# Key, query and value parts: from copies through DRAM to copies within SBUF

## The chip, the cores and the metric

The kernel runs on one core of one Trainium2 chip. The metric is the device time of one execution in microseconds (us), median of several runs. Engines are named TensorE (PE in the profile, its weight loads PEld), VectorE (DVE), ScalarE (ACT), GpSimd (POOL) and SyncE (SP); SyncE here does nothing but issue DMAs, in one order written out by hand.

## The reference, cut to what matters

32 items of 128 x 512 numbers go through a cross attention along the 512 positions (8 heads of 16 channels, keys and values from a second input) and then through a mixture of 8 experts with 2 chosen per token, plus a shared expert:

```
x   = x + tanh(g0) * attention(layernorm(x), ctx)     # per item: q, k, v = W @ x; scores over 512 x 512 per head;
                                                      # softmax; weighted values; 128 channels x 512 positions
x   = x + tanh(g1) * (moe(rmsnorm(layernorm(x))) + shared(rmsnorm(layernorm(x))))
```

The change is in the attention alone.

## The kernel before, in words

**Turns.** The attention runs in turns i = -3 to 31 (`TURNS`); an item is b. In turn i TensorE computes the transposed scores of item i (`exp_scores`, L882: 32 steps of four matmuls), their weighted sum with the values (`values`, L913), and, for item i+1, a first set of scores whose only use is the row maxima (`max_scores`, L860: 16 pairs of matmuls). VectorE takes the maxima of each pair (`maximum`, L1129), ScalarE the exponentials (`exponential`, L1413). Between them, at fixed steps s of the 32, lie the projections of item i+3 (`project`, L838; its value part, L844, is that of item i+2), their evacuation (`evacuate`, L1396 and L1400), the turning of the tokens of item i-3 and their router logits. All engines follow written orders and meet through semaphores; nothing is reordered at run time.

**Parts.** Keys and queries are cut into three bfloat16 parts, high, middle and low (`high_part` on ScalarE at steps 27 and 31 of turn b-3; the two others in `split` on GpSimd, L671 to L674: keys of item b near the end of turn b-3, queries at the start of turn b-2). The scores are one matmul over stacked parts: rows 0 to 47 of `k_stack` and `q_stack` hold 16 channels x 3 parts, and rows 64 to 111 the other three products; rows 32 to 63 hold also the constants and the maxima. Three stacks of each kind rotate (`b % 3`). [...]

**The way through DRAM.** `write` (L444) stores parts in `parts_d`: two DMAs of 256 KB for keys and two for queries per item. `read` (L458) loads them into the stacks: four DMAs of 192 KB for each. `max_scores` waits at its first step for all eight reads (`s_rd`). The maxima of an item come back as two rows of the query stack in `row` (L520), for half 0 before the turn of the item, for half 1 within it.

**The weighted values.** `take_values` (L1421) copies the sums of four heads, 16 value rows and 16 equal rows of denominators each, to `pv_sb`; `store_values` (L467) writes all 512 KB to `pv_d`, `spread_denominators` (L474) spreads four rows on 64 partitions for the reciprocal (`invert`), `store_reciprocals` (L478) writes them to DRAM, and `load_values` reads them back broadcast (L485) with the value rows (L486). `add_attention` on GpSimd (L681 to L683) waits for both.

**SyncE's order in turn i**, before: write(i+2, queries, HI); row(i, 1); spread_denominators(i-1); store_values(i-1); read(i+2, keys); write(i+2, queries, MID with LO); load_ctx, store_turned, load_x; row(i+1, 0); store_reciprocals(i-1); read(i+2, queries); load_values(i-1); store_tokens(i-2); store_staged, load_staged; write(i+3, keys, HI, then MID with LO). These are 28 DMAs. After the last turn come 71 jobs of matrix products, 32 of the shared expert and 39 of chosen ones (L956), which the change doesn't touch apart from the last item's values in jobs 0 to 4.

Of the kernel before, what the change touches and what calls it, by code (L numbers as in the profile page):

```python
# [7 lines left out]
F32 = mybir.dt.float32  # L8
# [20 lines left out]
STORED = ((LO, MID, HI, HI), (HI, HI, MID, LO))  # L29
HELD = ((HI, LO, MID), (HI, MID, LO))  # L30
FIRST_AT, SECOND_AT = (1, 0), (0, 1)
READS = 8
WRITES = 2
# [56 lines left out]
def build(nc, x_d, ctx_d, g_xattn_d, g_ffn_d, wq_d, bq_d, wk_d, bk_d, wv_d, bv_d, rms_d, router_d, w_d, out_d):  # L90
# [6 lines left out]
    with es:  # L97
# [50 lines left out]
        parts = [[held[n][:, HELD[n].index(part), :] for part in (HI, MID, LO)] for n in range(2)]  # L148
# [107 lines left out]
        parts_d = [[dram(f"parts_{n}{i}", (4, DH, HEADS, L), BF16) for i in range(2)] for n in "kq"]  # L256
        pv_d = dram("pv_d", (HEADS, 2 * DH, L), F32)
# [25 lines left out]
        s_wr = [sem(f"s_wr{i}") for i in range(2)]  # L283
        s_rd = [sem(f"s_rd{i}") for i in range(3)]
# [9 lines left out]
        s_w = sem("s_w")  # L294
# [102 lines left out]
        def lane(v, a):  # L397
            return v.rearrange("p (g a j) l -> p a g (j l)", g=2, a=2)[:, a, :, :]

        @block.sync  # L400
        def _(sp):
# [33 lines left out]
            def write(b, n, part):  # L435
                if b >= 2 and part == HI:
                    sp.wait_ge(s_rd[(b - 2) % 3], READS * DMA * ((b - 2) // 3 + 1))
                if part == HI:
                    sp.wait_ge(s_hi, 2 * b + n + 1)
                else:  # L440
                    sp.wait_ge(s_part, 4 * b + 2 * n + 2)
                rows = parts_d[n][b % 2].rearrange("t d h l -> (d h) t l")
                at = STORED[n].index(part if part == HI else HELD[n][1])
                sp.dma_start(rows[:, at:at + 2, :],  # L444
                             parts[n][HI].unsqueeze(1).broadcast_to([P, 2, L]) if part == HI else held[n][:, 1:3, :]
                             ).then_inc(s_wr[n], DMA)

            def read(b, n):
                sp.wait_ge(s_wr[n], WRITES * DMA * (b + 1))
                if b >= 3 and n == 0:  # L450
                    sp.wait_ge(s_es, STEPS * (b - 2))
                if b < 3 and n == 0:
                    sp.wait_ge(s_blank[b], 2)
                src = parts_d[n][b % 2]
                stack = (k_stack, q_stack)[n][b % 3]
                for a in range(2):
                    for row, at in ((LANE * a, FIRST_AT[n]), (LANE * (1 - a), SECOND_AT[n])):
                        sp.dma_start(lane(stack[row:row + STACK, :, :], a),  # L458
                                     lane(src[at:at + 3].rearrange("t d h l -> (t d) h l"), a)
                                     ).then_inc(s_rd[b % 3], DMA)  # L460

            def store_values(b):
                sp.wait_ge(s_u, 2 * b + 2)
                sp.wait_ge(s_fin, 2 * DMA * b)
                sp.dma_start(pv_d.rearrange("(g h) e l -> (h e) g l", g=2), pv_sb).then_inc(s_w, DMA)  # L467

            def spread_denominators(b):
                sp.wait_ge(s_u, 2 * b + 2)  # L470
                if b:
                    sp.wait_ge(s_rc, b)
                for g in range(2):
                    sp.dma_start(den_c[P // 2 * g:P // 2 * (g + 1), :], pv_sb[DH:P:2 * DH, g, :]).then_inc(s_sc, DMA)  # L474
# [5 lines left out]
            def load_values(b):  # L480
                sp.wait_ge(s_r, DMA * (b + 1))
                sp.wait_ge(s_w, DMA * (b + 1))
# [3 lines left out]
                sp.dma_start(pv_num, pv_d[:, 0:DH, :]).then_inc(s_fin, DMA)  # L486
# [36 lines left out]
            for i in TURNS:  # L523
                if is_b(i + 2):
                    write(i + 2, 1, HI)
# [1044 lines left out]
```

## Time and profile before

| | |
|---|---|
| median of 3 runs | 1391.8 us (1387.26, 1391.97, 1391.8) |
| the profiled execution | 1386.7 us, its span 1384.8 us |
| mean granted clock of TensorE | 0.983 of full speed |
| busy share: PE, DVE, ACT, POOL | 93%, 70%, 63%, 62% |
| DMA: MB moved, mean rate | 256.65 MB, 185 GB/s |
| DMA queue of SyncE | 149102 packets, 217.08 MB, 59.0% of 16 engines |

A busy TensorE is not TensorE at its peak, since matmuls are pipelined and their ends are modelled; so the waits say more than the share. Start times in the rows are us from the start of the span. A wait for several semaphores is put down to the one that came last.

### The profile page before, as it was taken

The numbers are of one execution on the slowest core, as the hardware profiler recorded it, in microseconds if no ns is written. First come the engines' busy times: TensorE is split into PE (matmuls) and PEld (weight loads), VectorE is DVE, ScalarE is ACT, GpSimd is POOL, SyncE is SP. The second block draws the span as 40 slices with busy tenths as digits, with TensorE's granted clock in tenths as the row PEclk, the third lists the DMA queues.
The fourth block names the chain that finished last, engine by engine and source line by source line (L and its number), as shares of the span: only waits on it lengthen the run. The fifth ranks groups of instructions, "written<-read, shape, count | busy, mean of one in ns | idle before, by whom it ended". The sixth has DMA issues, their size and how long they took to land.

```text
span 1384.8 us, 34397 instructions
## 1 busy us (share of the span) xinstructions
PE 1288.3 (93%) x12274; PEld 682.2 (49%) x12274; DVE 975.1 (70%) x1661; ACT 871.8 (63%) x1720; POOL 861.5 (62%) x1267
## 2 busy tenths in 40 slices
PE   2899999999999999999999989799999999999997
PEld 0233333333333333333333323587788888888886
DVE  5989889999999998989999877457654333333332
ACT  2488888888888888888888768333334333333332
POOL 8647777678787878877887643442114555555553
PEclk7799999999999999999999999999999999999999
DMA  7677887778888888788888773676555998885665
GB/s 187 185 197 227 224 241 220 207 227 214 201 223 207 213 218 227 191 222 210 218 217 221 162 185 90 161 161 149 127 175 105 214 216 193 178 189 110 108 110 81
DMA packets 167522, 256.65 MB, mean 185 GB/s; under 512 B 31717, under 2 KB 65132, under 8 KB 167358
## 3 DMA queue, kind: packets, MB, share of 16 engines
q1 hardware_dynamic: 149102, 217.08, 59.0%
q0 software_dynamic: 18256, 37.38, 14.9%
q8 instruction: 103, 1.69, 0.5%
q14 instruction: 61, 0.50, 0.1%
HBM read 141.06 MB, written 112.27 MB: 183 GB/s over the span
## 4 chain that ended last, share of the span: by engine, by line
PE 61%; DVE 12%; issue 10%; DMA 7%; POOL 3%; ACT 3%; SPq 2%; POOLq 1%; DVEq 0%; ACTq 0%
PE m_banks L956 21%; PE bank L913 12%; PE bank L882 10%; DVE row_max L1129 8%; PE m_banks L860 7%; PE bank L838 3%; PE bank L888 3%; DMA arena<-parts_q 2%; PE bank L844 2%; ACT arena L1413 2%; DMA arena<-ht_d 1%; POOL xs L780 1%; PE bank L978 1%; SPq L458 1%; PE bank L869 1%
## 5 line engine op out<-in xcount | busy, mean ns | idle before, releaser
L1129 DVE TENSOR_REDUCE row_max<-m_banks 128x2 f32<-128x1024 f32 x512 | 615.0, 1222 | 76.1 <-PE m_banks L860 67.9
L1413 ACT ACTIVATE arena<-bank 128x512 f32<-128x512 f32 x1024 | 552.4, 606 | 73.4 <-PE bank L882 71.9
L882 PE MATMUL bank<-arena 112*32 112x512 bf16 x4096 | 336.2, 382 | 6.6 <-ACT arena L1413 3.2
L913 PE MATMUL bank<-arena 128*32 128x512 f32 x2048 | 280.2, 598 | 0.4 <-ACT arena L1421 0.3
L882 PEld LDWEIGHTS bank<-arena 112*32 112x32 bf16 x4096 | 114.7, 95 | 266.0 <-ACT arena L1413 132.4
L792 POOL DMA_INDIRECT out<-xs,ids x71 | 112.3, 1582 | 173.4 <-ACT xs L1495 135.7
L860 PE MATMUL m_banks<-arena 48*128 48x512 bf16 x1024 | 177.4, 393 | 39.6 <-DVE row_max L1129 25.7
L956 PE MATMUL m_banks<-w_ring,h_hi 128*128 x568 | 183.0, 403 | 0.0
L1484 ACT ACTIVATE arena<-m_banks 128x256 f32<-128x256 f32 x103 | 39.5, 384 | 186.9 <-PE m_banks L956 186.9
L860 PEld LDWEIGHTS m_banks<-arena 48*128 48x128 bf16 x1024 | 40.4, 93 | 175.2 <-DVE row_max L1129 79.9
L1337 DVE TENSOR_TENSOR arena<-arena,m_banks 128x256 f32<-128x256 f32 x71 | 29.9, 421 | 116.5 <-ACT arena L1484 116.5
L956 PE MATMUL m_banks<-w_ring,h_lo 128*128 x284 | 111.7, 393 | 0.0
L956 PEld LDWEIGHTS m_banks<-w_ring,h_hi 128*128 128x128 f32 x568 | 101.4, 189 | 18.4
L671 POOL TENSOR_TENSOR arena<-arena 128x512 bf16<-128x512 f32 x62 | 72.2, 1165 | 49.8 <-ACT arena L1405 46.7
L1331 DVE TENSOR_TENSOR act_lo<-bank,act_hi 128x256 fp32r<-128x256 f32 x71 | 30.1, 424 | 96.7 <-ACT act_hi L1501 96.7
L681 POOL TENSOR_TENSOR arena<-arena 128x512 f32<-128x512 f32 x32 | 40.9, 1277 | 89.9 <-DMA arena<-pv_d 86.9
L780 POOL DMA_INDIRECT xs<-h_d,ids x71 | 70.2, 989 | 41.0 <-issue 21.0
L732 POOL DMA_INDIRECT map_d<-meta,slots x64 | 65.5, 1023 | 47.2 <-DVE slots L1216 31.4
L1495 ACT ACTIVATE xs<-m_banks,wts 128x512 f32<-128x512 f32 x71 | 48.8, 688 | 71.0 <-PE m_banks L956 71.0
L913 PEld LDWEIGHTS bank<-arena 128*32 128x32 f32 x2048 | 64.8, 109 | 49.6 <-issue 26.5
L956 PE MATMUL m_banks<-w_ring,act_hi 128*128 x284 | 87.5, 389 | 1.4 <-DVE act_lo L1331 1.4
L838 PE MATMUL bank<-arena 128*32 128x512 f32 x512 | 72.1, 636 | 16.4 <-POOL arena L662 11.1
(182 smaller groups left out, 1999.9 us busy)
## 6 DMA issues: line engine op xcount, KB each, us to landing
arena<-parts_k SPq DMA_DIRECT2D x128, 192.0 KB
arena<-parts_q SPq DMA_DIRECT2D x128, 192.0 KB
parts_k<-arena SPq DMA_DIRECT2D x64, 256.0 KB, 6.6
parts_q<-arena SPq DMA_DIRECT2D x64, 256.0 KB, 5.1
pv_d<-arena SPq DMA_DIRECT2D x32, 512.0 KB, 4.3
split_d<-staged SPq DMA_DIRECT2D x30, 512.0 KB, 9.1
w_ring<-split_d SPq DMA_DIRECT2D x60, 256.0 KB, 3.9
arena<-in_w SPq DMA_DIRECT2D x36, 256.0 KB, 8.4
```

Source lines behind the costliest of these rows:

```text
L671: nc.gpsimd.tensor_tensor(mid, proj[n], hi, ALU.subtract).then_inc(s_part, 1)
L732: nc.gpsimd.indirect_dma_start(map_d, bass.IndirectOffsetOnAxis(ap=slots[:, k, b:b + 1], axis=0), meta[:, k, b, :], None).then_inc(s_sc2, DMA)
L780: nc.gpsimd.indirect_dma_start(gathered[i % IN_RING], None, h_d, bass.IndirectOffsetOnAxis(ap=ids[:, i:i + 1], axis=0)).then_inc(s_got[i % ...
L792: nc.gpsimd.indirect_dma_start(out_d, bass.IndirectOffsetOnAxis(ap=ids[:, i:i + 1], axis=0), y_sb[i % OUT_RING], None, compute_op=ALU.add) ...
L838: last = nc.tensor.matmul(out[c, :], (wk, wq)[n][:, c], ctx_in[b % 2] if n == 0 else xn[b % 2], start=True, stop=True)
L860: nc.tensor.matmul(m_ps[pair % M_PAIRS][:, a, :], q_stack[b % 3][rows, h, qt * P:(qt + 1) * P], k_stack[b % 3][rows, h, :], start=True, st ...
L882: last = nc.tensor.matmul(out[c, :], k_stack[b % 3][0:SHIFTED, h, kt * P + c.start:kt * P + c.stop], q_stack[b % 3][0:SHIFTED, h, :], star ...
L913: last = nc.tensor.matmul(pv_ps[2 * DH * j:2 * DH * (j + 1), :], v_ones[b % 3][:, kt, GROUP * g + j, :], probs[pair % 3][:, j, :], start=( ...
L956: last = nc.tensor.matmul(out, v[:, c, :], weights(j, part, first_row + c), start=(c == 0 and n == 0), stop=(c == chunks - 1 and n == 2))
L1129: nc.vector.reduce_max(pair, m_ps[(STEPS * b + u) // 2 % M_PAIRS], AX_X).then_inc(s_mx, 1)
L1413: nc.scalar.activation(probs[group % 3][:, j, :], bank_of["scores", b, s], ACT.Exp, scale=float(DH) ** -0.5).then_inc(s_exp, 1)
L1495: nc.scalar.activation(y_sb[i % OUT_RING], Y_PS[j % 2], ACT.Copy, scale=wts[:, i:i + 1]).then_inc(s_yrt, 1)
```

## The change

Each part is copied straight from where `split` and `high_part` leave it into the rows of the stacks. The stacks interleave the three parts of a channel now (every third row), so each copy writes 16 partitions, 3 apart, x 8 or 4 heads x 512. Keys take 10 copies an item and queries 8: six of 128 KB and twelve of 64 KB. All of an item's are issued in turn b-2: the high key parts first of all in the turn, the rest after `spread_denominators`. The value rows and rows of ones of `v_ones` alternate, and `send_values` copies the 128 value rows (2 x 128 KB) straight to `pv_num`; the 512 KB store and the 256 KB load are gone. The reciprocals go through DRAM as before. `parts_d` and `pv_d` are gone. Neighbouring heads (a) lie on the two halves of the partitions now, where pairs of heads did.

```diff
-READS = 8
-WRITES = 2
+SLOTS_OF = (((HI, HI), (HI, MID), (MID, LO)), ((HI, LO), (MID, MID), (HI, HI)))
+COPIES = tuple(sum(2 if first == second else 4 for first, second in slots) for slots in SLOTS_OF)
...
+            def copy_parts(b, n, part):
                 if part == HI:
+                    if n == 0:
+                        if b >= 3:
+                            sp.wait_ge(s_es, STEPS * (b - 2))
+                        if b < 3:
+                            sp.wait_ge(s_blank[b], 2)
                     sp.wait_ge(s_hi, 2 * b + n + 1)
+                if part == MID:
                     sp.wait_ge(s_part, 4 * b + 2 * n + 2)
+                stack, src = (k_stack, q_stack)[n][b % 3], parts[n][part]
+                for at, (first, second) in enumerate(SLOTS_OF[n]):
+                    for base in (0, LANE):
+                        rows = stack[base + at:base + at + STACK - 2:len(SLOTS_OF[n]), :, :]
+                        if part == first == second:
+                            sp.dma_start(rows, src).then_inc(s_cp[n], DMA)
+                        else:
+                            for a in range(2):
+                                if part == (first if base == LANE * a else second):
+                                    sp.dma_start(rows[:, a:HEADS:2, :], src[a:P:2, :]).then_inc(s_cp[n], DMA)
+
+            def send_values(b):
                 sp.wait_ge(s_u, 2 * b + 2)
+                if b:
+                    sp.wait_ge(s_x2, b)
+                for g in range(2):
+                    sp.dma_start(pv_num[P // 2 * g:P // 2 * (g + 1), :], pv_sb[0:P:2, g, :]).then_inc(s_num, DMA)
...
             for i in TURNS:
                 if is_b(i + 2):
-                    write(i + 2, 1, HI)
+                    copy_parts(i + 2, 0, HI)
                 if is_b(i):
                     row(i, 1)
                 if is_b(i - 1):
                     spread_denominators(i - 1)
-                    store_values(i - 1)
                 if is_b(i + 2):
-                    if i + 2 > 0:
-                        read(i + 2, 0)
-                    write(i + 2, 1, MID)
-                    if i + 2 == 0:
-                        read(0, 0)
+                    copy_parts(i + 2, 0, MID)
+                    copy_parts(i + 2, 0, LO)
+                    for part in (HI, MID, LO):
+                        copy_parts(i + 2, 1, part)
+                if is_b(i - 1):
+                    send_values(i - 1)
...
                 if is_b(i - 1):
                     store_reciprocals(i - 1)
-                if is_b(i + 2):
-                    read(i + 2, 1)
                 if is_b(i - 1):
-                    load_values(i - 1)
+                    load_reciprocals(i - 1)
...
-                if is_b(i + 3):
-                    for part in (HI, MID):
-                        write(i + 3, 0, part)
...
             def split(b, n):
...
-                pool.wait_ge(s_wr[n], WRITES * DMA * b)
+                pool.wait_ge(s_cp[n], COPIES[n] * DMA * b)
...
             def add_attention(b):
-                pool.wait_ge(s_fin, 2 * DMA * (b + 1))
+                pool.wait_ge(s_num, 2 * DMA * (b + 1))
+                pool.wait_ge(s_fin, DMA * (b + 1))
...
             def max_scores(b, u):
                 if u == 0:
-                    pe.wait_ge(s_rd[b % 3], READS * DMA * (b // 3 + 1))
+                    for kind in range(2):
+                        pe.wait_ge(s_cp[kind], COPIES[kind] * DMA * (b + 1))
...
             def evacuate(b, n):
-                        act_e.wait_ge(s_wr[n], WRITES * DMA * b)
+                        act_e.wait_ge(s_cp[n], COPIES[n] * DMA * b)
...
-                nc.scalar.copy(v_ones[b % 3][:, :, :, 0:DH],
+                nc.scalar.copy(v_ones[b % 3][:, :, :, 0::2],
```

## Rows read from the trace of the kernel before

**Rows 1.** The page: busy time by engine, and the chain that ended last.
```profile
PE 1288.3 (93%) x12274; PEld 682.2 (49%) x12274; DVE 975.1 (70%) x1661; ACT 871.8 (63%) x1720; POOL 861.5 (62%) x1267
...
PE 61%; DVE 12%; issue 10%; DMA 7%; POOL 3%; ACT 3%; SPq 2%; POOLq 1%; DVEq 0%; ACTq 0%
```

**Rows 2.** Windows: opening, turns 5 to 28, and a half-clock stretch of turn 30.
```profile
core 0: us, PE busy (x) PEld busy (x) DVE busy (x) ACT busy (x) POOL busy (x), PEclk, DMA share, GB/s
...
12.50:14.00 1.50, 0.66 (x4) 0.20 (x8) 0.00 (x0) 0.00 (x0) 1.42 (x3) 1.00 1.06 377
20.50:31.50 11.00, 1.99 (x10) 0.29 (x12) 3.47 (x17) 1.30 (x2) 9.11 (x21) 0.50 0.95 199
826.10:832.90 6.80, 5.91 (x38) 1.76 (x42) 3.14 (x5) 2.38 (x5) 1.70 (x2) 0.50 0.60 173
174.20:823.50 649.30, 613.34 (x7801) 219.16 (x7797) 592.48 (x950) 532.13 (x1028) 501.70 (x830) 1.00 0.81 212
```

**Rows 3.** Waits over turns 5 to 28: total us, times, longest.
```profile
PEld bank L882 <- ACT arena L1413: 97.1, 300, 0.5
...
POOL arena L681 <- DMA arena<-pv_d: 42.4, 21, 5.3
...
PEld bank L882 <- DMA arena<-m_rows: 3.9, 5, 1.9
PE m_banks L860 <- DMA arena<-parts_q: 3.0, 2, 1.5
```

**Rows 4.** The same view over the whole run.
```profile
PE m_banks L860 <- DMA arena<-parts_q: 13.2, 5, 6.5
```

**Rows 5.** Timeline of TensorE where turns 4, 5 and 21 begin.
```profile
149.14 0.61 PE L882 MATMUL bank<-arena 112*32 112x512 bf16 x8
...
174.24 0.61 PE L882 MATMUL bank<-arena 112*32 112x512 bf16 x8
...
589.36 0.62 PE L882 MATMUL bank<-arena 112*32 112x512 bf16 x8
591.46 0.61 PE L860 MATMUL m_banks<-arena 48*128 48x512 bf16 x4 [1.49 <-DMA arena<-parts_q]
```

**Rows 6.** The chain that ended last, opening: start us, us, what.
```profile
18.76 0.36 SPq L444
...
24.35 7.05 DMA arena<-parts_q
...
45.02 0.56 SPq L520
```

**Rows 7.** Timeline of the opening: TensorE, then GpSimd.
```profile
23.02 1.94 PE L838 MATMUL bank<-arena 128*32 128x512 f32 x8 [5.03 <-POOL arena L662]
31.44 1.04 PE L860 MATMUL m_banks<-arena 48*128 48x512 bf16 x4 [6.49 <-DMA arena<-parts_q]
...
51.84 0.61 PE L882 MATMUL bank<-arena 112*32 112x512 bf16 x8
53.29 0.61 PE L860 MATMUL m_banks<-arena 48*128 48x512 bf16 x4 [0.85 <-DMA arena<-parts_q]
...
32.62 1.15 POOL L674 TENSOR_TENSOR arena<-arena 128x512 bf16<-128x512 f32 x1
...
36.34 1.15 POOL L674 TENSOR_TENSOR arena<-arena 128x512 bf16<-128x512 f32 x1
```

**Rows 8.** Timeline of SyncE's DMA queue in turn 20: start us, us.
```profile
568.17 1.20 SPq L520 DMA_DIRECT2D arena<-m_rows  x2
...
571.71 3.33 SPq L458 DMA_DIRECT2D arena<-parts_k  x4
...
580.21 1.17 SPq L520 DMA_DIRECT2D arena<-m_rows  x2
...
582.04 3.07 SPq L458 DMA_DIRECT2D arena<-parts_q  x4
585.23 0.65 SPq L485 DMA_DIRECT2D arena<-rden_d  x1
```

More of the change, by code:

```diff
@@ L147, in build @@
         held = [a.take(3 * L // 2, BF16).rearrange("p (t l) -> p t l", t=3) for _ in range(2)]
-        parts = [[held[n][:, HELD[n].index(part), :] for part in (HI, MID, LO)] for n in range(2)]
+        parts = [[held[n][:, part, :] for part in (HI, MID, LO)] for n in range(2)]
         wq, wk, wv = (a.take(P) for _ in range(3))
@@ L253, in build @@
         bank_of = {}
-        parts_d = [[dram(f"parts_{n}{i}", (4, DH, HEADS, L), BF16) for i in range(2)] for n in "kq"]
-        pv_d = dram("pv_d", (HEADS, 2 * DH, L), F32)
         rden_d = dram("rden_d", (HEADS, L), F32)
@@ L282, in build @@
         s_part = sem("s_part")
-        s_wr = [sem(f"s_wr{i}") for i in range(2)]
-        s_rd = [sem(f"s_rd{i}") for i in range(3)]
+        s_cp = [sem(f"s_cp{i}") for i in range(2)]
         s_ms = sem("s_ms")
@@ L441, in write @@
                     sp.wait_ge(s_part, 4 * b + 2 * n + 2)
[L442 to L460, printed above, removed]
@@ L473, in spread_denominators @@
                 for g in range(2):
-                    sp.dma_start(den_c[P // 2 * g:P // 2 * (g + 1), :], pv_sb[DH:P:2 * DH, g, :]).then_inc(s_sc, DMA)
+                    sp.dma_start(den_c[P // 2 * g:P // 2 * (g + 1), :], pv_sb[1:P:2 * DH, g, :]).then_inc(s_sc, DMA)
             def store_reciprocals(b):
@@ L478, in store_reciprocals, with load_reciprocals @@
                 sp.dma_start(rden_d, rden_c).then_inc(s_r, DMA)
-            def load_values(b):
+            def load_reciprocals(b):
                 sp.wait_ge(s_r, DMA * (b + 1))
-                sp.wait_ge(s_w, DMA * (b + 1))
                 if b:
@@ L741, in _ @@
             for n in (1, 2):
-                link(nc.gpsimd.memset(v_ones[n][:, :, :, DH:], 1.0))
+                link(nc.gpsimd.memset(v_ones[n][:, :, :, 1::2], 1.0))
                 nc.gpsimd.memset(middle_rows(k_stack[n]), TWO_ONES).then_inc(s_blank[n], 1)
@@ L858, in max_scores @@
                 for a in range(2):
-                    rows, h = slice(LANE * a, LANE * a + STACK), GROUP * g + 2 * a + j
+                    rows, h = slice(LANE * a, LANE * a + STACK), GROUP * g + 2 * j + a
                     nc.tensor.matmul(m_ps[pair % M_PAIRS][:, a, :], q_stack[b % 3][rows, h, qt * P:(qt + 1) * P],
@@ L1127, in maximum @@
                 half, w = divmod(u // 2, GROUP * KT // 2)
-                pair = row_max[b % 2][:, GROUP * KT * half:GROUP * KT * (half + 1)].rearrange("p (a w) -> p w a", a=2)[:, w, :]
+                pair = row_max[b % 2][:, GROUP * KT * half:GROUP * KT * (half + 1)].rearrange("p (j a t) -> p j t a", a=2, t=KT)[:, w // KT, w % KT, :]
                 nc.vector.reduce_max(pair, m_ps[(STEPS * b + u) // 2 % M_PAIRS], AX_X).then_inc(s_mx, 1)
@@ L1144, in _ @@
             nc.vector.memset(middle_rows(k_stack[0]), TWO_ONES).then_inc(s_blank[0], 1)
-            nc.vector.memset(v_ones[0][:, :, :, DH:], 1.0).then_inc(s_ones, 1)
+            nc.vector.memset(v_ones[0][:, :, :, 1::2], 1.0).then_inc(s_ones, 1)
             run(moments(0))
@@ L1418, in take_values @@
                 if b:
-                    act_e.wait_ge(s_w, DMA * b)
+                    act_e.wait_ge(s_num, 2 * DMA * b)
                     act_e.wait_ge(s_sc, 2 * DMA * b)
```

19 lines of the change are left out of this document (3 added, 16 removed).

## The prediction, made before the change was run

> **What bounds the kernel now.** The page comes first. TensorE is busy 93% of the span and has 61% of the chain that ended last, while DMA as a whole has 7% of that chain [rows 1]. So taking traffic away pays only where a transfer is what TensorE waits for. The window of turns 5 to 28 sizes the attention: 802 exponentials were counted there, or 25.06 turns in 649.3 us, which makes 25.91 us a turn, and TensorE is busy in 613.34 us of it [rows 2]. A turn without a disturbance, turn 4, takes 174.24 - 149.14 = 25.10 us [rows 5]. The DMA engines are busy 0.81 of that window at 212 GB/s [rows 2]: nearly full, and yet seldom waited for. The waits tell why. In 25 turns TensorE waits 97.1 us for exponentials in small pieces, which is the pace of the turn itself, but only 3.0 us for query parts, and its weight loads wait 3.9 us for maxima rows [rows 3]. The reader is to see that steady turns are set by the interplay of TensorE, ScalarE and VectorE. Over the whole run the wait for query parts is 13.2 us in 5 cases [rows 4]. The opening holds two of them: 6.49 us before turn -1's first maxima matmul at 31.44, and 0.85 us at 53.29 [rows 7]. Turn 21 has one of 1.49 [rows 5], another of that size makes up the 3.0, and 13.2 - 6.49 - 0.85 - 3.0 leaves 2.9 us for a later one, at turn 30. The removal of these waits is what the change can bring.
>
> **The opening.** The last query parts of item 0 exist at about 18.7: their store is issued at 18.76. Key reads, then query reads follow, the last issued at 24.35, and it lands 7.05 us later [rows 6]. The copies need no second trip. High query parts go ahead of that time; after 18.76 four copies are left, at 0.6 us an issue (x2 in 1.20, x4 in 3.33 or 3.07 with some crowding [rows 8]), so the last is issued at about 21.2. Queries are 768 KB; at the 199 GB/s of the stretch 20.5 to 31.5, where these very stack rows are written from DRAM [rows 2], that takes 3.9 us and is paced by the issues. I take a landing by 24.5. TensorE is then not ready either: the projection at 23.02 ends at 24.96 and itself waited for GpSimd [rows 7]. Turn -1's maxima start at 25.0 instead of 31.44: 6.4 us won. With the old 7.05 us of landing it would be 28.3, and 3.1 us.
>
> Turn -1 is then a row of maxima on VectorE, unchanged. It would put the start of turn 0 at 45.4 instead of 51.84. Its first scores need row(0, 0). That was issued at 45.02 when the maxima were there [rows 6], which becomes 38.6, but now eighteen copies of item 1 stand ahead of it in SyncE's order. GpSimd finishes item 1's key parts at 33.8 and its query parts at 37.5 [rows 7], times that don't move, since its work there is continuous. Six key copies run to 37.4, four high query copies to 39.8, four more to 42.2, load_ctx to 42.9; the row goes out by 44.1 and I take 2 us to land: 46.1, 0.7 us after the start it could have had (between 0 and 3). The 0.85 us wait for item 1 goes. TensorE's granted clock was half from 20.5 to 31.5 [rows 2]; where it returns moves with the work, and I charge 1 us, between 0 and 3.4: half of the 6.8 us that one half-clock stretch lasted [rows 2]. Opening: 6.4 + 0.85 - 0.7 - 1.0 = 5.6 us won, bounds 0 and 7.3.
>
> **Steady turns.** Before, the last query read of turn 20 ends its issue at 585.11, about 4 us before the next turn at 589.36, whose first maxima wait for it [rows 5, 8]. The copies are issued in one block: high keys at 0 to 2.4 us of the turn, row(i, 1) at 4 as before, the denominators to 6.5, fourteen copies to 15 or 16. The last goes out some 5 us before the old one did. The waits of 3.0 + 2.9 = 5.9 us fall away; at worst they stay. The maxima rows stand behind less traffic: of their 3.9 us I take half, 2.0 (0 to 3.9).
>
> Traffic: 1.05 MB of stores, 0.5 MB of value stores and 0.26 MB of loads go; 1.57 MB of reads turn into copies of as many bytes and 0.26 MB of value copies come. The stores ran at 377 GB/s [rows 2], so some 4 us of 21 us of DMA time a turn are freed. Nothing waits for that time by itself. GpSimd's 42.4 us for pv_d [rows 3] shrink, since only the reciprocals are left to wait for. GpSimd is off the path: I count 0. The upper bound is half of what turns 5 to 28 hold above 25.10 us after the waits named: (0.81 x 25 - 6.9) / 2 = 6.7 us.
>
> The new stops. The copies have a new place in `evacuate`: ScalarE must wait until all of the previous item's copies have landed, with the exponentials queued behind it and TensorE behind those. The query evacuation is at step 29, about 22.8 us of the turn; copies issued by 16 have 6 us and more to land. Cost nothing while that cover stands. The writes with stride 2 into `v_ones` have the same 512 elements a row, and I count 0. No row has the stride. If it doubled such a copy, that would be 532.13 / 1028 = 0.52 us a turn on an engine that is idle (649.30 - 532.13) / 25 = 4.7 us of each [rows 2], so 0 to 0.5 us a turn, and I take the lower end.
>
> **The issue queue.** SyncE had 28 DMAs a turn and gets 28 - 12 - 2 + 18 + 2 = 34. At 0.6 us that is 20.4 instead of 16.8 us. Waits that remain: 1.6 us for the maxima before row(i, 1), and now the landing of the reciprocals. The query reads used to lie in that gap, and 582.0 to 585.23 sufficed [rows 8], so at most 3.2 us. 20.4 + 1.6 + 3.2 = 25.2 against 25.9: it fits, but barely. row(i+1, 0) goes out some 2 us later than its 16 us of the turn, and still has 6.
>
> A rule of the Trainium skill speaks against this cut into pieces: "SBUF — State Buffer", section on the DMA setup-cost knee, has small transfers dominated by a fixed part, 64 KB moving at about 138 GB/s. By an estimate from that page, twelve such copies and six of 128 KB take some 10 us a turn, about what stores and reads took together, and it would not change the sum. No row of before has such a copy.
>
> **The sum.** 5.6 + 5.9 + 2.0 = 13.5 us. The profiled execution took 1386.7 (span 1384.8), so it would be 1373.2. The median of the runs is 5.1 us above the profiled time; against 1391.8 it is 1378.3, and I say 1378. Its own range, from the bounds: 1368 to 1386.
>
> **Rivals.** *Only the opening pays.* The late waits are an accident of how DMAs fell in three turns, and others come in their place, for a maxima row or a landing. For it: two of the three lie among the last turns, where shared weights are loaded too. Against: the copies lead by 5 us. Time: 1391.8 - 5 = 1387, within 0.5%. Chance 0.20.
>
> *SyncE becomes the bound* (the other side). An issue of a copy with two strided sides could take longer than 0.6; the four reads took up to 0.83 each in 571.71 [rows 8]. The room is 0.7 us, and the wait of 1.6 us would shrink before the turn grows, so it decides from 0.6 + 2.3 / 18 = 0.73 us a copy; each further 0.1 adds 1.8 us a turn. At 0.83 that is 1.8 x 28 turns = 50, less the 13.5: 1428. For it: how little room there is. Against: an average of 0.6 for transfers with as many dimensions. Chance 0.11.
>
> *The copies clog the DMA engines.* A turn moves 212 x 25.91 = 5.5 MB; without stores, reads and value traffic, and with the value copies, 2.35 MB are left, 6.2 us at 377 GB/s. The copies would have to fall from 199 to under 1.57 / 19.7 = 80 GB/s to fill the turn. Neither a 1 KB piece (the stores had them, at 377) nor the stack rows (199) come near. At 70 GB/s: 2.7 us x 28 = 76, less 13.5: 1454. Chance 0.06.
>
> **How the numbers follow.** The forecast has 0.63. Faster by over 0.5% means under 1384.8; 7 us is what this measurement can tell from none, with runs 4.7 us apart. Nearly all of the forecast is that (0.60), and a small part of the first rival (0.04): 0.64. Same: 0.03 and 0.15, so 0.18. Slower: 0.17 and a little of the first rival: 0.18. The range must leave out at most 2 in 10: 1368 to 1395, which leaves the two slow rivals outside.
>
> **What would show it.** Right: no L860 wait on a DMA at turns 21, 29, 30; the first L860 at about 25; turn 0 near 46; SyncE's row(i+1, 0) at 18 us of a turn; 32 x 1.57 = 50 MB less moved; GpSimd's L681 waiting little. Wrong: copy issues above 0.7 us; L520 released late, followed by L882 waiting for m_rows; L1396 waiting for a DMA; a turn mean above 25.9; half clock in turn 0.

## The result: 8% slower, and the profile after

The changed kernel takes 1502.6 us, the median of 4 runs (1498.6 to 1506.3), against 1389.5 for 4 runs of the kernel before: a ratio of 1.080 [1.076, 1.085]. The profiled execution took 1498.57 us with a span of 1496.7, at a mean granted clock of 0.947 where before had 0.983.

The page of the kernel after: span, busy time by engine, the DMA totals, the chain that ended last, and one of the costliest groups (busy us and mean ns, then idle time before it, and from what).

```profile
span 1496.7 us, 34532 instructions
...
PE 1328.1 (89%) x12274; PEld 682.8 (46%) x12274; DVE 976.7 (65%) x1661; ACT 875.2 (58%) x1720; POOL 860.3 (57%) x1267
...
DMA packets 154468, 206.34 MB, mean 138 GB/s; under 512 B 35046, under 2 KB 84845, under 8 KB 154303
...
PE 40%; SPq 26%; DMA 10%; issue 10%; DVE 7%; POOL 5%; ACT 2%; POOLq 1%; ACTq 0%; DVEq 0%
...
L1401 ACT COPY arena<-bank 128x512 f32<-128x512 f32 x64 | 37.3, 583 | 103.3 <-DMA arena<-arena 102.1
```

The traffic did what was said: 256.65 MB became 206.34, so 50.3 MB are gone. Every engine does the work that it did before [rows 1]; TensorE's busy time is 3.1% longer, 39.8 us for the same instructions at a lower mean clock; the others' is within 0.4%. The other 72.1 of the 111.9 us between the spans are standing time of TensorE. In the chain TensorE fell from 61% to 40% and SyncE's queue rose from 2% to 26%. The last row names the place: ScalarE's 64 copies in `take_values` have 102.1 us of idle time in front of them, released by DMAs between buffers on chip.

The window view of the kernel after, of its exponentials alone (32 a turn): turns 5 to 28, turn 15, and a stretch of turn 17.

```profile
core 0: us, ACT busy (x), PEclk, DMA share, GB/s
193.38:916.00 722.62, 413.01 (x768) 0.94 0.47 132
497.50:525.50 28.00, 17.59 (x34) 1.00 0.55 152
578.00:584.50 6.50, 2.67 (x5) 0.50 0.37 121
```

The first row holds 768 exponentials, so 24 turns, in 722.62 us: 30.11 us a turn, where before it was 25.91 [rows 2]. Turn 15 takes 28.00 us at full clock. The last row is a stretch at half clock, begun 20 us into turn 17, and 17 of the 24 turns have one. The seven others take 27.8 to 28.5 us, 28.1 on average; the 17 average (722.6 - 7 x 28.1) / 17 = 30.9. Of the 4.2 us that a turn has grown, 2.2 are there without any half clock, and 2.0 come with it.

The attention holds the whole loss. The last four exponentials of turn 31 start in the timeline of ScalarE after at:

```profile
990.47 2.06 ACT L1393 ACTIVATE arena<-bank 128x512 f32<-128x512 f32 x4 [3.09 <-PE bank L862]
```

Before, the row is:

```profile
873.48 2.06 ACT L1413 ACTIVATE arena<-bank 128x512 f32<-128x512 f32 x4 [2.80 <-PE bank L882]
```

That is 117.0 us later. Behind it each kernel has some 510 us left (1384.8 - 873.5 = 511.3, 1496.7 - 990.5 = 506.2), so the jobs give back 5 us, and 117.0 - 5.1 is the 111.9 us between the two spans.

**Where a turn stands still.** The waits of the kernel after from 174 to 900 us, some 24 turns (total us, times, longest):

```profile
POOL arena L649 <- ACT arena L1385: 148.1, 24, 11.3
...
PE bank L893 <- ACT arena L1401: 87.2, 24, 5.1
ACT arena L1401 <- DMA arena<-arena: 85.0, 24, 5.0
```

No maxima matmul waits for a transfer any more, as forecast [rows 3, 4]. But ScalarE waits 85.0 us in 24 turns for a copy between buffers, 3.5 us on average and 2.6 to 5.0 in each, and TensorE's value matmuls wait 87.2 us for ScalarE. One wait passes through to the other whole. GpSimd's wait follows from it: it stands idle until ScalarE has made the next high part, later in the turn than before. Turn 15, which starts at 497.5, shows how it comes about. SyncE's queue in the timeline (start us, us):

```profile
501.40 1.18 SPq L503 DMA_DIRECT2D arena<-m_rows  x2
502.67 1.25 SPq L459 DMA_DIRECT2D arena<-arena  x2
503.97 5.08 SPq L445 DMA_DIRECT2D arena<-arena  x8
509.09 3.14 SPq L441 DMA_DIRECT2D arena<-arena  x4
512.27 1.25 SPq L445 DMA_DIRECT2D arena<-arena  x2
513.62 1.17 SPq L452 DMA_DIRECT2D arena<-arena  x2
...
516.44 1.22 SPq L503 DMA_DIRECT2D arena<-m_rows  x2
517.70 0.58 SPq L463 DMA_DIRECT2D rden_d<-arena  x1
521.94 0.66 SPq L469 DMA_DIRECT2D arena<-rden_d  x1
...
524.66 3.34 SPq L441 DMA_DIRECT2D arena<-arena  x2
```

The order of the turn can be read down the list. The maxima row goes out 3.9 us into the turn, when VectorE has it, then `spread_denominators` (L459), fourteen part copies until 513.5, and only then `send_values` (L452). Behind those come the three 256 KB transfers, row(16, 0), and `store_reciprocals` (L463). The load of the reciprocals (L469) starts 3.66 us after that store's issue ended, and the next turn's high keys at 524.66. The same turn on ScalarE, and then on TensorE:

```profile
513.89 0.60 ACT L1393 ACTIVATE arena<-bank 128x512 f32<-128x512 f32 x1 [1.15 <-PE bank L862]
517.09 0.59 ACT L1401 COPY arena<-bank 128x512 f32<-128x512 f32 x1 [2.60 <-DMA arena<-arena]
...
517.82 1.06 PE L893 MATMUL bank<-arena 128*32 128x512 f32 x8 [2.69 <-ACT arena L1401]
```

ScalarE was free at 514.49, 17.0 us into the turn. Its next instruction is `take_values(15, 0)` at step 20. This overwrites `pv_sb`, from which `send_values(14)` reads, and those two copies were issued at 513.62 and landed at about 517.0. ScalarE stands for 2.60 us, exponentials of the steps behind it are queued on the same engine, and TensorE stands for 2.69. The next turn then starts later by about that much: turn 15 takes 28.0 us, turn 4 before took 25.1 [rows 5]. SyncE's order, which is tied to the turn's start by row(i, 1), moves with it, and the wait is met again in every turn from 1 to 29: 102.1 us in all. Turn 15 is one of the milder cases.

### The profile page after: what moved, and what is told of

Its sections match the earlier page's. It is cut to its first block, busy times and chain, and to the rows that moved or that the text cites. A ratio compares the mean times of both kernels' runs of the same rounds, so it can differ in the third digit from the quotient of the medians.

```text
span 1496.7 us, 34532 instructions
## 1 busy us (share of the span) xinstructions
PE 1328.1 (89%) x12274; PEld 682.8 (46%) x12274; DVE 976.7 (65%) x1661; ACT 875.2 (58%) x1720; POOL 860.3 (57%) x1267
## 2 busy tenths in 40 slices
DMA packets 154468, 206.34 MB, mean 138 GB/s; under 512 B 35046, under 2 KB 84845, under 8 KB 154303
## 4 chain that ended last, share of the span: by engine, by line
PE 40%; SPq 26%; DMA 10%; issue 10%; DVE 7%; POOL 5%; ACT 2%; POOLq 1%; ACTq 0%; DVEq 0%
PE m_banks L936 20%; SPq L445 14%; PE bank L893 6%; SPq L441 6%; DMA arena<-arena 5%; PE bank L862 5%; PE bank L817 4%; DVE row_max L1109 4%; PE m_banks L840 3%; SPq L503 2%; SPq L459 2%; DMA rden_d<-arena 2%; SPq L452 2%; PE bank L868 1%; DMA arena<-rden_d 1%
## 5 line engine op out<-in xcount | busy, mean ns | idle before, releaser
L893 PE MATMUL bank<-arena 128*32 128x512 f32 x2048 | 294.8, 629 | 105.0 <-ACT arena L1401 104.9
L862 PE MATMUL bank<-arena 112*32 112x512 bf16 x4096 | 349.3, 395 | 8.9 <-ACT arena L1393 5.8
L862 PEld LDWEIGHTS bank<-arena 112*32 112x32 bf16 x4096 | 119.1, 98 | 295.1 <-ACT arena L1393 155.1
L817 PE MATMUL bank<-arena 128*32 128x512 f32 x512 | 86.0, 752 | 15.9 <-POOL arena L640 10.6
L840 PEld LDWEIGHTS m_banks<-arena 48*128 48x128 bf16 x1024 | 37.1, 95 | 137.3 <-issue 87.8
L1401 ACT COPY arena<-bank 128x512 f32<-128x512 f32 x64 | 37.3, 583 | 103.3 <-DMA arena<-arena 102.1
L1311 DVE TENSOR_TENSOR act_lo<-bank,act_hi 128x256 fp32r<-128x256 f32 x71 | 30.1, 424 | 96.7 <-ACT act_hi L1481 96.7
L711 POOL DMA_INDIRECT map_d<-meta,slots x64 | 65.3, 1021 | 47.3 <-DVE slots L1196 30.9
```

What stands on the lines that cost most here:

```text
L817: last = nc.tensor.matmul(out[c, :], (wk, wq)[n][:, c], ctx_in[b % 2] if n == 0 else xn[b % 2], start=True, stop=True)
L840: nc.tensor.matmul(m_ps[pair % M_PAIRS][:, a, :], q_stack[b % 3][rows, h, qt * P:(qt + 1) * P], k_stack[b % 3][rows, h, :], start=True, st ...
L862: last = nc.tensor.matmul(out[c, :], k_stack[b % 3][0:SHIFTED, h, kt * P + c.start:kt * P + c.stop], q_stack[b % 3][0:SHIFTED, h, :], star ...
L893: last = nc.tensor.matmul(pv_ps[2 * DH * j:2 * DH * (j + 1), :], v_ones[b % 3][:, kt, GROUP * g + j, :], probs[pair % 3][:, j, :], start=( ...
```

## The experiments

The ratios are to the kernel before, measured beside each run; the intervals are 95%. None leaves work out; three add some. A maxima row that is late is waited for by the weight loads and then by the matmuls behind them; the two rows of a view overlap, so they are not added up. First came the place of `send_values` in the order, with one edit each: 0, 6 or 10 part copies ahead of it in its block instead of 14.

### Values first

```diff
                 if is_b(i - 1):
                     spread_denominators(i - 1)
+                    send_values(i - 1)
...
-                if is_b(i - 1):
-                    send_values(i - 1)
```

> The value copies stand right behind the spreading of the denominators instead of behind fourteen part copies; nothing else differs from the changed kernel. Theory A (their place: ScalarE's first taking of values in a turn waits for the value copies of the item before to land): that taking returns from about 20 to about 17 us of a turn, a turn takes 25.5 to 26.5 us, the kernel 1375 to 1400 us. Theory B (SyncE has too many issues, 34 a turn): the order changes nothing, 1470 to 1505 us. Theory C (copies within SBUF are slow in the DMA engines): likewise above 1470 us, with landings of parts far above 3 us.

Measured: 1388.2 us, ratio 1.002 [0.999, 1.004]. ScalarE's wait for copies is gone, and with it the loss of 8%. A turn takes 26.6 us on average in turns 5 to 28, a little more than expected. It may not be the best place: SyncE itself stands 20.8 us in 14 turns for GpSimd, which still reads `pv_num`, and TensorE's weight loads wait 18.0 us for maxima rows.

### Values after the key copies, and after ten copies

```diff
                     copy_parts(i + 2, 0, MID)
                     copy_parts(i + 2, 0, LO)
-                    for part in (HI, MID, LO):
-                        copy_parts(i + 2, 1, part)
                 if is_b(i - 1):
                     send_values(i - 1)
+                if is_b(i + 2):
+                    for part in (HI, MID, LO):
+                        copy_parts(i + 2, 1, part)
```

> The value copies stand behind six part copies (the middle and low key parts), 3.7 us later than in the run with none ahead. Theory A: they are issued at 10 to 11 us of the turn and land by 14, before step 20 at about 16.5, so the time is that of the run with none ahead, within 8 us. Were every place in the queue worth its 0.62 us, it would be 6 x 0.62 x 28 = 104 us above that one. Theories B and C: about 1500 us, as the changed kernel.

Measured with six copies ahead: 1383.7 us, ratio 0.996 [0.994, 0.999].

The next one puts the four high query copies ahead of `send_values` as well:

```diff
                     copy_parts(i + 2, 0, LO)
+                    copy_parts(i + 2, 1, HI)
                 if is_b(i - 1):
                     send_values(i - 1)
                 if is_b(i + 2):
-                    for part in (HI, MID, LO):
+                    for part in (MID, LO):
                         copy_parts(i + 2, 1, part)
```

> The value copies stand behind ten part copies. Theory A: issued by 14 us of the turn, landing at about 16.5, at the edge: 0 to 1 us a turn, so 0 to 28 us above the run with six ahead, where fourteen ahead cost over 100 us. The cost is a threshold, not a slope from the first copy. Theories B and C: about 1500 us.

Measured with ten ahead: 1404.8 us, ratio 1.012 [1.008, 1.015]. Its wait of `take_values` for copies, over 174 to 850 us:

```profile
ACT arena L1403 <- DMA arena<-arena: 38.0, 22, 4.4
```

In the same stretch the wait is 0 with none ahead, 3.4 us with six, 38.0 with ten and 82.5 with fourteen, at ratios of 1.002, 0.996, 1.012 and 1.080. The traffic, the copies and the number of issues are the same in all four. That leaves the order as the cause. The four copies from six to ten cost 2.5 us of issue each turn, and six copies ahead is about where the landing meets its user just in time. The time lost is not in proportion to the wait: from six to ten copies 34.6 us more of it go with 21 us, from ten to fourteen 44.5 with 98.

### A second buffer, with the order of the change

```diff
+        second_half = arena[:, a.at:a.at + L]
...
+        def pv_half(b, g):
+            return second_half if g == 0 and b % 2 else pv_sb[:, g, :]
...
             def take_values(b, g):
-                if b:
-                    act_e.wait_ge(s_num, 2 * DMA * b)
-                    act_e.wait_ge(s_sc, 2 * DMA * b)
-                nc.scalar.copy(pv_sb[:, g, :], pv_ps).then_inc(s_u, 1)
+                sent = b if g else b - 1
+                if sent > 0:
+                    act_e.wait_ge(s_num, 2 * DMA * sent)
+                    act_e.wait_ge(s_sc, 2 * DMA * sent)
+                nc.scalar.copy(pv_half(b, g), pv_ps).then_inc(s_u, 1)
```

> The changed kernel in its own order, the value copies behind fourteen part copies, but the first half of the weighted values of odd items goes to a second buffer, so that the taking at step 20 waits only for the copies of two items before. Theory A (the wait of ScalarE on that landing is the cost, not the late issue): the waits of ScalarE on a DMA vanish, 1378 to 1400 us. Theory B (the queue as such is too long) or C: stays above 1450 us. Waits for maxima rows may remain and make up 10 to 20 us.

`send_values` stays behind fourteen copies. Only the first half of an odd item's values goes to another buffer, so that the taking at step 20 has to wait for the item before the last one. Measured: 1386.0 us, ratio 0.996 [0.993, 0.999]. `take_values` waits for no DMA. This settles it: with the issue order of the change untouched, taking away what makes ScalarE wait takes the 8% away. What is late instead (174 to 850 us):

```profile
POOL arena L664 <- DMA arena<-rden_d: 86.0, 23, 8.6
...
PEld bank L866 <- DMA arena<-m_rows: 26.1, 14, 6.4
...
PE bank L866 <- DMA arena<-m_rows: 16.8, 9, 5.5
```

GpSimd waits 86.0 us for the reciprocals, and TensorE's weight loads wait 26.1 us for maxima rows, with the matmuls' 16.8 inside that. Even so the kernel ends 0.4% under the one before.

### The two halves of the change alone

Values through DRAM again, at the old place and with the old store and load; parts by copies (34 issues a turn):

```diff
                 if is_b(i - 1):
                     spread_denominators(i - 1)
+                    store_values(i - 1)
...
-                if is_b(i - 1):
-                    send_values(i - 1)
```

> Only the parts go by copies within SBUF; the weighted values go through DRAM, with their store at its old place and their load behind that of the reciprocals. SyncE has 34 issues a turn, as in the changed kernel. Theory A: ScalarE waits only for the early store, so a turn takes 25.5 to 26.5 us and the kernel 1375 to 1400 us. Theory B (34 issues are too many): about 1500 us. Theory C: about 1500 us.

Measured: 1379.7 us, ratio 0.996 [0.993, 0.999], against 1385.9 beside it.

The kernel before, with only the values by copies, in the place of its store (28 issues):

```diff
                 if is_b(i - 1):
                     spread_denominators(i - 1)
-                    store_values(i - 1)
+                    send_values(i - 1)
```

> The kernel before, with only the weighted values sent by copies within SBUF, at the place where their store stood. 28 issues a turn, as before. Values direct by themselves gain nothing, since no wait of TensorE hung on them: 1378 to 1392 us, same as before within 0.5%. If ScalarE's stop on the landing of the values were costly wherever they stand, it would show here too: above 1400 us.

Measured: 1388.0 us, ratio 0.998 [0.995, 1.001]. Neither half is slow by itself. The parts alone bring 6 us, about the opening, and the values alone nothing that can be told from none.

### The clock kept up through the wait

```diff
+            def keep_busy(b, u, count):
+                pair = (STEPS * b + u) // 2
+                pe.wait_ge(s_mx, pair - M_PAIRS + 1)
+                for _ in range(count):
+                    nc.tensor.matmul(m_ps[pair % M_PAIRS][:, 0, :], q_stack[b % 3][0:STACK, 0, 0:P],
+                                     k_stack[b % 3][0:STACK, 0, :], start=True, stop=True)
...
+                    if s == 20 and is_b(i) and i and is_b(i + 1):
+                        keep_busy(i + 1, s + GROUP, 14)
```

> The changed kernel with 14 added matmuls (48 rows, 128 x 512, 3 us at full clock) in each turn right ahead of the weighted values at step 20, where TensorE stands waiting; their results are overwritten. In the changed kernel 22 of 31 turns held 3.4 or 6.8 us at half clock and took 30 to 33 us, those without took 27.8 to 28.5. If the clock is half of the loss: half-clock time in the turns falls from 126 us to under 20, turns to 28.0 to 28.8, the kernel 1440 to 1460 us. If the clock costs nothing beside the wait, the added work is hidden or added: 1500 us or up to 30 us more.

The order is the change's; fourteen matmuls whose result is overwritten stand where TensorE would wait. Measured: 1501.6 us, ratio 1.079 [1.074, 1.083]: by the number the second expectation, though the clock did come back in part. TensorE's timeline in such a turn:

```profile
510.37 3.19 PE L847 MATMUL m_banks<-arena 48*128 48x512 bf16 x14 [0.59 <-DVE row_max L1118]
513.87 1.06 PE L900 MATMUL bank<-arena 128*32 128x512 f32 x8 [0.31 <-ACT arena L1410]
```

The gap is filled: 0.59 and 0.31 us of idling stand where turn 15 had 2.69, and no turn from 1 to 30 has a gap of TensorE over 1.1 us. ScalarE's wait stays (80.8 us). The mean granted clock rises from 0.947 to 0.961 only, and the time not at all. If the clock is at one of its two levels, its half-speed share is 2 x (1 - mean): 159 us of the span after, 117 here, 47 before. The added matmuls took back 42 us of half clock; in turns 0 to 30 it is 92 us of 126, where the first expectation had under 20. In turns 5 to 28 those without any half clock take 28.9 us on average instead of 28.1, and the mean over all 24 is 30.2 instead of 30.1: the added work costs what the clock gives back. The clock still fell in 17 of the turns 1 to 30, so TensorE's standing is not what it needs to fall.

The lengths of the turns within this run price the half clock. Against the 11 without it (28.9 us), the 6 with a stretch of 3.4 us take 1.5 us more and the 7 with 6.8 us take 3.1 more, so about half its length. By that, an estimate, the 92 us of half clock in turns 5 to 28 of the changed kernel are worth some 42 us, 1.8 of the 4.2 us that a turn has grown. It compares turns and is not a test of its own.

Nor does the length of a wait decide: in the changed kernel the clock stayed at full behind 3.33 us of standing in turn 21 and fell behind 2.62 in turn 3.

### Does the number of issues matter by itself?

The kernel before with six tiny DMAs more a turn (34, as after):

```diff
                     write(i + 2, 1, MID)
...
+                    for k in range(6):
+                        sp.dma_start(extra_d[i + 2, k], ident[0:16, 0:8]).then_inc(s_extra, DMA)
```

> The kernel before with six more DMAs of 512 bytes a turn (34 issues, as many as the changed kernel), issued right behind the store of the middle query parts; they write to DRAM what nobody reads. If 34 issues are too many for SyncE in themselves: every turn grows and the kernel takes more than 1450 us. If they fit and only what stands behind them comes later (the maxima rows by up to 1 us, the query reads by some): 1388 to 1410 us.

Measured: 1418.7 us, ratio 1.022 [1.018, 1.026]. Its waits for the query parts (174 to 850 us):

```profile
PEld m_banks L866 <- DMA arena<-parts_q: 24.4, 16, 5.6
...
PE m_banks L866 <- DMA arena<-parts_q: 19.1, 13, 5.1
```

The matmuls' 19.1 us lie within the weight loads' 24.4; before had 5.9 and 7.8 in the same stretch. The time lies between the two expectations, above 1410 and far below 1450. The six issues took 2.80 us of the queue in one turn, and before had less room than that in front of its last reads. So issues do cost, when they stand ahead of something that is needed soon.

### An order that puts what is late first

Six copies, `send_values`, six query copies, `store_reciprocals`, the last two query copies, row(i+1, 0), `load_reciprocals`, and only then the three 256 KB transfers:

```diff
                 if is_b(i + 2):
-                    for part in (HI, MID, LO):
-                        copy_parts(i + 2, 1, part)
+                    copy_parts(i + 2, 1, HI)
+                    copy_parts(i + 2, 1, MID)
+                if is_b(i - 1):
+                    store_reciprocals(i - 1)
+                if is_b(i + 2):
+                    copy_parts(i + 2, 1, LO)
+                if is_b(i + 1):
+                    row(i + 1, 0)
+                if is_b(i - 1):
+                    load_reciprocals(i - 1)
                 if is_b(i + 4) and i + 4 >= 2:
                     load_ctx(i + 4)
...
-                if is_b(i + 1):
-                    row(i + 1, 0)
-                if is_b(i - 1):
-                    store_reciprocals(i - 1)
-                if is_b(i - 1):
-                    load_reciprocals(i - 1)
```

> Against the order with the values behind six part copies: the reciprocals are stored before the last two query copies, the maxima rows of the next item go out right behind those copies, and the loads of context and x and the store of turned tokens come last. What the run with six ahead still showed was TensorE waiting 10.7 us for maxima rows over 25 turns and GpSimd 61 us for reciprocals. Theory A with this remainder (the 34 issues fit, the urgent ones must stand first): the waits for maxima rows fall under 3 us, the turn mean to 25.7 to 26.1 us, the kernel 1368 to 1378 us. Theory B in its weak form (34 issues with copies are at their limit whatever the order): the waits only move elsewhere and the time stays at 1380 to 1388 us.

Measured: 1366.3 us, ratio 0.982 [0.979, 0.985]: faster than both kernels, 24.6 us below before and 9% below the change. That is a little better than expected, but not for the reason given: the weight loads' wait for maxima rows did not fall under 3 us, it is 10.3 where the order with six ahead has 7.7. SyncE's own waits, first of the kernel after (174 to 850 us):

```profile
SPq L469 <- DMA rden_d<-arena: 79.0, 22, 8.1
SPq L503 <- DVE m_rows L1119: 31.1, 20, 2.4
```

and of this one:

```profile
SPq L503 <- DVE m_rows L1122: 54.9, 27, 6.0
...
SPq L469 <- DMA rden_d<-arena: 0.5, 1, 0.5
```

The 79.0 us in which the whole queue stood for the reciprocals' way through DRAM are 0.5, since two copies and the row are issued meanwhile. The only long wait left is for the maxima themselves, as before.

Two runs asked which of the moves brings it. This order differs from the one with six ahead in three places: the store of the reciprocals, their load, and row(i+1, 0). Only the row moved, from the order with six copies ahead:

```diff
                         copy_parts(i + 2, 1, part)
+                if is_b(i + 1):
+                    row(i + 1, 0)
...
-                if is_b(i + 1):
-                    row(i + 1, 0)
```

> The order with the values behind six part copies, and one more move: the maxima rows of the next item are issued before the loads of context and x and the store of turned tokens instead of behind them; the reciprocals stay where they were. If the rows' lateness (10.7 us of TensorE's waits over 25 turns) was what kept that version at 0.9963 of the time before: most of the way to the reordered version, 1368 to 1376 us. If the reciprocals' way (61 us of GpSimd's waits, and the query parts that GpSimd makes later for it) was: 1378 to 1386 us.

Measured: 1415.8 us, ratio 1.018 [1.014, 1.021], against both expectations. The store of the reciprocals now stands directly behind the three 256 KB transfers. SyncE waits for it before the next turn's work, and row(i, 1) of that turn is late, 12 to 15 us in:

```profile
SPq L469 <- DMA rden_d<-arena: 74.5, 18, 7.2
```

```profile
PEld bank L863 <- DMA arena<-m_rows: 22.7, 12, 3.3
...
PE bank L863 <- DMA arena<-m_rows: 12.9, 10, 2.3
```

Only the store of the reciprocals moved:

```diff
+                    copy_parts(i + 2, 1, HI)
+                    copy_parts(i + 2, 1, MID)
+                if is_b(i - 1):
+                    store_reciprocals(i - 1)
+                if is_b(i + 2):
+                    copy_parts(i + 2, 1, LO)
```

> The order with the values behind six part copies, with one move: the reciprocals are stored before the last two query copies instead of behind the maxima rows; their loading, the rows and the loads of context and x stay where they were. In the version without this move SyncE stood 55.7 us over 25 turns waiting for the reciprocals to land in DRAM, and moving the rows alone made it 1416 us. If that round trip is what bound the queue: SyncE's wait for it falls under 5 us, the kernel comes to 1362 to 1374 us, the time of the fully reordered version. If both moves are needed: 1376 to 1386 us.

Measured: 1392.5 us, ratio 1.005 [1.002, 1.009], again against both. SyncE no longer waits for the reciprocals, but row(i+1, 0) still stands behind the 256 KB transfers, and TensorE waits for it:

```profile
PEld bank L865 <- DMA arena<-m_rows: 31.2, 14, 5.2
...
PE bank L865 <- DMA arena<-m_rows: 21.2, 9, 4.3
```

By their ratios, one move alone costs 2.1% or 0.9% against the order that it started from (0.996), 30 or 13 us; both, with the load of the reciprocals moved as well, win 1.5%, 20 us. I did not foresee that. The waits suggest why: each alone leaves something needed soon behind the big transfers. They are not the whole of it, since the row moved also went with 34 us of half clock in turns 5 to 28, where six ahead has 3. The two moves without that of the load were not run, so how much of the gain is the load's is open.

The last run gives the good order six tiny DMAs more a turn (40), ahead of `send_values`:

```diff
                     copy_parts(i + 2, 0, LO)
+                    for k in range(6):
+                        sp.dma_start(extra_d[i + 2, k], ident[0:16, 0:8]).then_inc(s_extra, DMA)
                 if is_b(i - 1):
                     send_values(i - 1)
```

> The reordered version with six more DMAs of 512 bytes a turn, 40 issues, placed between the key copies and the value copies; they write to DRAM what nobody reads. SyncE's own time becomes 40 x 0.62 = 25 us of a turn of 25.7. Theory of a full queue: all stands later by 3.7 us, the values land at the edge of step 20 and the maxima rows after it: a turn of 27 to 28 us, the kernel 1400 to 1440 us. If SyncE's issues cost nothing as long as the order is right: under 1380 us.

Measured: 1459.4 us, ratio 1.049 [1.045, 1.053], above what was expected. The first wait is back (174 to 850 us):

```profile
ACT arena L1410 <- DMA arena<-arena: 44.7, 24, 3.8
```

Pushing the value copies back by some 2.8 us brings ScalarE's wait again, with something else than part copies ahead of them. It does not price that wait: 38.0 us of it with ten copies ahead went with 21 us over six ahead, and here 93 us are lost. Weight loads also wait 27.2 us for rows, and how much is due to the count of 40 is left open.

## Why the prediction was wrong, step by step

**The opening: right.** TensorE's timeline after:

```profile
22.95 1.94 PE L817 MATMUL bank<-arena 128*32 128x512 f32 x8 [4.58 <-POOL arena L640]
24.81 1.04 PE L840 MATMUL m_banks<-arena 48*128 48x512 bf16 x4
...
46.58 0.62 PE L862 MATMUL bank<-arena 112*32 112x512 bf16 x8 [0.89 <-DMA arena<-m_rows]
```

The first maxima matmul starts at 24.81 (said: 25.0; before 31.44 [rows 7]) with nothing to wait for, since the projection ends just then. Turn 0 starts at 46.58 (said: 46.1), 0.89 us of it waiting for row(0, 0) (said: 0.7), and 5.3 us before the old one (said: 5.6 with the clock's part).

**The waits for parts: right.** None is left, neither in the turns nor at turns 29 and 30. Whether their 5.9 us became time cannot be read from the changed kernel. The parts alone brought 6.2 us of 1385.9 in all, and 5.1 of it is the opening (turn 0 at 46.76).

**The price of an issue: right, within 7%.** Of turn 15's copies eight took 5.08 us and two 1.25, so 0.62 to 0.64 us each. The fourteen were out 16.0 us into the turn (said: 15 or 16). The copies land fast; from the page of the kernel after (KB, median us from issue to landing):

```profile
arena<-arena SPq DMA_DIRECT2D x256, 128.0 KB, 2.9
arena<-arena SPq DMA_DIRECT2D x384, 64.0 KB, 2.1
```

So they did not clog the DMA engines; that rival is out. The Trainium skill ("DMA: Bandwidth & Descriptors", the section on the anatomy of one DMA, on the path of DMAs that GpSimd issues) gives each transfer a fixed part of about 2.0 us, mostly the write's receipt, and bytes at 436 GB/s on top. These copies are issued by SyncE. By an estimate from that page 64 KB take 2.15 us, near the 2.1 of the row, and 128 KB 2.3, which is 0.6 too little here.

**The new stops: the step that failed.** The prediction named one new wait of a compute engine for landings, that of `evacuate`, and gave it 6 us of cover. That cover stood: in the changed kernel `evacuate` waits for no copy; only with 40 issues a turn does it, 7.8 us in 5 cases. Its stride of 2 into `v_ones` is real but small, 646 ns a copy where before had 586. But the prediction never named the other wait that the diff shows, that of `take_values` for `s_num`. Before, the 512 KB store of the values was issued ahead of the parts, and its landing covered; the change puts the copies that replace it behind fourteen others. The prediction's own numbers would have priced it: copies out by 16 us, 1.2 us of issue for `send_values`, some 2 us of landing, so 19.2 us at the earliest. In turn 20 of the kernel before TensorE begins and ScalarE takes the values at:

```profile
564.11 0.80 PE L882 MATMUL bank<-arena 112*32 112x512 bf16 x8
```

```profile
580.71 0.58 ACT L1421 COPY arena<-bank 128x512 f32<-128x512 f32 x1
```

That is 16.6 us into the turn, so the wait would have come out at 2.6 us a turn, 73 us over the 28 turns that the prediction counts with. It measured 3.5 us on average, 102.1 in all; that turn 15 shows just 2.60 is luck. The half clock comes on top, by the estimate above. The prediction asked "who waits" of the parts and GpSimd's `pv_num`, but not of the buffer that the copies read from: the program lets nobody overwrite the source of a copy before it has landed.

**The issue queue: a size too small, and a wrong place to look.** The landing of the reciprocals was bounded at 3.2 us. SyncE's wait for it is 79.0 us in 22 cases, 3.6 on average and 8.1 at most. The sum of 25.2 us against 25.9 still said "it fits", and it did in the sense meant: the rival in which the price of SyncE's issues sets the turn was not the loss, since SyncE itself has 7 us of waits a turn (79.0 + 31.1 above, with 29.0 and 24.0 for two others, over 22.5 turns). Whether the queue is full says little. What decides is when its order reaches each transfer that has a user with a fixed time.

**The maxima rows and GpSimd.** With the loss in place TensorE hardly waited for a row. Without it the rows are the next thing late: the weight loads wait 7.7 us with six copies ahead, 10.3 reordered, 22.7 with the row moved, 26.1 with the second buffer, 31.2 with the early reciprocals, where before had 3.9. The forecast had 2.0 us won there. GpSimd was taken as without price. No run tests that, but its waits for the reciprocals do not follow the time: 9.3 us in the changed kernel, at 1.080, and 86.0 with the second buffer at 0.996.

**The range.** "From the bounds" the prediction's own range goes to 1386. Its bounds give more: with nothing won in the opening and the waits left as they were, the upper end is 1391.8. The lower bound of 0 in the opening is not the sum of its terms either (3.1 won with the old landing, less up to 3 and 3.4). Neither mattered beside the wait that was left out.

**What stays open.** Why the granted clock falls 19 to 22 us into many turns, even with the gap filled. What the half clock costs by itself is an estimate from turn lengths, since the run meant to separate it from the wait did not. Where all of the reordered kernel's 24.6 us comes from is also open. In its profiled execution, itself 8.5 us above its median, the opening gives 5.6 us (turn 0 at 46.29 instead of 51.84), the turns 3 and the jobs 3 more. Its turns 5 to 28 are no shorter than before's (26.2 us on average against 26.0); turn 30 is, 23.6 against 29.0, since before had a wait and half clock there. And the saved 50 MB were never seen to pay by themselves.

## What to carry to other kernels

When a transfer is moved in a hand-written queue, list everything that waits for its landing: the reader of the target, and the engine that next overwrites the source. Price each against the time at which that engine has come there before. A queue with time to spare can still be late for one user, and a short wait ahead of an in-order engine's main work repeats in every turn; so order the queue by who is late next, small transfers with near users ahead of large ones without. Measure such moves together as well as singly: each of two moves alone was a loss here, where the order that had both, and a third, gained.

## What the runs showed of the hardware that was not expected

- A ScalarE copy that writes every second element of 512 took 646 ns against 586.
- Copies within SBUF landed in 2.1 us (64 KB, 64 rows to every third of 48) and 2.9 us (128 KB, the value copies among them), and cost SyncE 0.62 to 0.64 us of issue each in turn 15; plain tiny stores to DRAM cost 0.47 (2.80 us for six).
- The order with six copies ahead (0.996) went to 1.018 and 1.005 with one of two moves made, and to 0.982 with both and the load of the reciprocals moved.
- A stand of TensorE of 2.6 to 5.1 us in each turn went with three times the half clock (159 against 47 us of the span). Fourteen matmuls in its place took only 42 us of that back, and without any gap over 1.1 us the clock fell in 17 of 30 turns.
